# Averages as 32-column tiles on TensorE, and five of twelve key units a batch turned by TensorE instead of by DMA

## The chip, the cores and the metric

The kernel runs on one core of a Trainium2 chip: TensorE (matrix products, into PSUM), VectorE, ScalarE and GpSimd (elementwise work), SyncE, whose queue here issues all DMA transfers, and 16 DMA engines behind it. The metric is the device time of one execution in microseconds; lower is better.

## The reference

Two stages follow one another. The first is two cross-attention layers (16 heads of width 128) and an MLP over `x` [8, 56, 256] with the context `ctx` [8, 1500, 256]. The second, which this text calls the audio stage, is one more cross-attention with 16 heads of width 16 over the same context:

```python
a = layer_norm(audio_kv, ln_gamma, ln_beta)                      # [8, 1500, 256]
Q = (hidden @ Wq.T).reshape(B, 56, 16, 16).transpose(0, 2, 1, 3)
K = (a @ Wk.T).reshape(B, 1500, 16, 16).transpose(0, 2, 1, 3)
V = (a @ Wv.T).reshape(B, 1500, 16, 16).transpose(0, 2, 1, 3)
scores = einsum('bhtd,bhsd->bhts', Q, K) * 16 ** -0.5            # masked, all true here
attn = softmax(scores, axis=-1)
out = einsum('bhts,bhsd->bhtd', attn, V)                         # [8, 16, 56, 16]
result = hidden + tanh(gate) * (out.reshape(B, 56, 256) @ Wo.T)
```

## The kernel before

All products are made in float16 with operands split into a high and a low half, so that most of them are made two or three times.

The audio stage has eight batches. In each, the 16 heads x 56 queries are 896 rows, cut into seven tiles of 128 rows, and the 1500 keys are cut into twelve units of 128. The heads fall into four windows of four heads (224 rows), numbered w = 0 to 3. A unit is one key block's keys and values, 512 columns: six matmuls (`unit`), then `unit_high` on ScalarE and `unit_low` on VectorE write its two halves to the buffer `core`, the values to a ring of 33 slots and the keys to a ring of six.

The program runs tile by tile; tile y = 7 b + s stands in slot s of batch b. In each slot

- TensorE (`audio_attention` in the tensor block) makes the scores of tile y into three PSUM banks SC (six matmuls of 512 columns, twelve where two windows meet, `audio_scores`), then units of the next batch, and in four of the seven slots an average: probabilities times values for one window (`audio_average`);
- VectorE makes the masked minimum of the scores (`audio_minimum`, L1616), the low half of the previous tile's probabilities (`audio_low`, L1634), the low halves of units (L1675) and the softmax scale (L1623, L1625);
- ScalarE converts the previous tile's probabilities (`audio_high`, L1346), picks an average out of PSUM (`pick_average`, L1354), takes the exponential (`audio_exponentiate`, L1337), and makes the high halves of units (`unit_high`, L1330). Two passes over the mask (L1361, L1367) stand in slots 3 and 5;
- the SP queue issues the transposing DMAs: both halves of the previous tile's probabilities (`turn_audio`, L560 and L562, twelve 128 x 128 blocks each), and in slots 0, 2, 4 and 5 the keys of three units of the next batch (`turn_keys`, L551), which the scores need with the key index along the columns; then the loads of the batch after.

The order inside a slot is written out by hand, and each engine runs its own in order. Tables say which slot does what: `SLOT_UNITS` the units, `SLOT_KEYS` the key transposes, `SLOT_WINDOWS` the averages (window 0 in slot 4, 1 in slot 6, 2 and 3 in slots 1 and 2 of the next batch), `SLOT_PICKS` the picks.

An average multiplies 128 value columns (four heads, each with a high and a low half of 16) with all 224 rows of the window. Of the [128, 224] result only four blocks of 32 x 56 are wanted, a head's own columns against its own queries, and a pick reads each with an activation of its own. The averages of windows 0 and 2 go to PSUM bank PV[0], those of 1 and 3 to PV[1].

L791 is the line of the helper `mm`, in which all matmuls are recorded.

## Time and profile before

| what | us |
|---|---|
| median of the three runs (1451.38 to 1454.85) | 1454.21 |
| profiled execution, its own time | 1454.63 |
| its span | 1452.7 |
| audio stage, first minimum to the end | 1126.8 to 1452.7 |
| TensorE busy over the span | 1408.5 (97%) |
| VectorE, ScalarE, GpSimd busy | 988.7, 869.5, 480.2 |

Times in the rows below are from the start of the span. A busy time is a sum of instruction durations, and on TensorE the instructions overlap: the pitch between starts, not the duration of one, is what a matmul takes in a row of them. "Idle before" is the time the engine stood still ahead of a group, with what ended it.

### The profile page before, as it was taken

Reading aid. Unit: us, or ns where it says so; the run is one execution under the profiler, and the core shown is the slowest. Engines: PE = TensorE matmul, PEld = TensorE weight load, DVE = VectorE, ACT = ScalarE, POOL = GpSimd, SP = SyncE. Lnnn points to the kernel's source line nnn. Section 1 sums busy time; section 2 is a strip of 40 time slices with the busy share of each in tenths; the row PEclk is TensorE's granted clock in tenths of the full one; section 3 lists DMA queues with packets and bytes.
Section 4 is the critical chain, followed back from the end, with each engine's and each line's share of the span. In section 5 each row is a group of like instructions: output and inputs, shape, how many; then the busy total and the mean of one; then the engine's idle time right before and its main releaser. Section 6 shows DMA issues by size and latency. Waiting matters only on the chain.

```text
span 1452.7 us, 24712 instructions
## 1 busy us (share of the span) xinstructions
PE 1408.5 (97%) x9188; PEld 888.8 (61%) x9188; DVE 988.7 (68%) x2030; ACT 869.5 (60%) x1566; POOL 480.2 (33%) x393
## 2 busy tenths in 40 slices
PE   9999999999999999999999999999899999999987
PEld 5466666666666654566666666667554455555545
DVE  6866555555555658867666666665657988879886
ACT  6755545545545547655455455455445888988886
POOL 5545433434434200235434433420011443333300
PEclk9999999999999999999999999999999999999999
DMA  6399988889988721599899899987612899999998
GB/s 213 92 228 201 184 171 182 178 171 182 176 173 182 159 88 30 133 219 191 183 178 169 184 177 168 181 163 152 184 41 55 166 219 210 216 209 216 221 199 158
DMA packets 671058, 246.88 MB, mean 170 GB/s; under 512 B 643692, under 2 KB 645212, under 8 KB 670940
## 3 DMA queue, kind: packets, MB, share of 16 engines
q1 hardware_dynamic: 670940, 245.32, 83.4%
q8 instruction: 73, 1.20, 0.3%
q14 instruction: 45, 0.37, 0.1%
HBM read 85.28 MB, written 0.52 MB: 59 GB/s over the span
## 4 chain that ended last, share of the span: by engine, by line
PE 75%; DVE 8%; DMA 7%; ACT 6%; issue 3%; SPq 1%; DVEq 0%; ACTq 0%; POOL 0%; POOLq 0%
PE SC L791 40%; PE PV L791 35%; DMA core<-qc 4%; DVE qc L1634 2%; DVE prob L1616 2%; ACT qc L1346 2%; ACT prob L1337 1%; DMA qc<-core 1%; DVE core L1675 1%; ACT core L1330 1%; DMA core<-core 1%; ACT small L1354 1%; DMA core<-in_wv_dram 1%; ACT rowbuf L1361 0%; SPq L560 0%
## 5 line engine op out<-in xcount | busy, mean ns | idle before, releaser
L791 PE MATMUL PV<-core 128*128 128x256 f16 (+1 forms) x4800 | 540.6, 270 | 14.2 <-DMA core<-qc 6.4
L791 PEld LDWEIGHTS PV<-core 128*128 128x128 f16 x4800 | 458.5, 98 | 83.9 <-issue 15.0
L1278 ACT ACTIVATE prob<-SC,core 128x500 f32<-128x500 f32 x336 | 223.9, 675 | 409.1 <-DVE core L1640 408.4
L791 PE MATMUL SC<-ctxT,qc 128*128 128x500 f16 x2016 | 443.4, 374 | 0.0
L1609 DVE TENSOR_REDUCE mx<-SC 128x1 f32<-128x500 f32 x330 | 220.9, 669 | 316.0 <-PE SC L791 316.0
L791 PEld LDWEIGHTS SC<-ctxT,qc 128*128 128x128 f16 x2016 | 195.9, 97 | 206.9
L719 POOL CAST ctxT<-stage 128x750 f16<-128x750 f32 x64 | 66.9, 1045 | 431.1 <-PE SC L791 223.5
L1667 DVE SCALAR_TENSOR_TENSOR core<-prob,core 128x1500 f16<-128x1500 f32 x112 | 198.4, 1771 | 4.3 <-ACT core L1287 4.3
L1287 ACT ACTIVATE core<-prob 128x1500 f16<-128x1500 f32 x112 | 162.7, 1453 | 3.6
L791 PE MATMUL SC<-ctxT 128*128 128x512 f16 x552 | 131.0, 380 | 4.6 <-DVE core L1675 4.6
L791 PE MATMUL SC<-qc 128*128 128x512 f16 x480 | 114.4, 383 | 12.9 <-DVE mx L1616 12.9
L723 POOL TENSOR_TENSOR core<-stage,core 128x768 f16<-128x768 f32 x64 | 108.0, 1688 | 9.0 <-DVE core L1486 4.1
L1634 DVE SCALAR_TENSOR_TENSOR qc<-prob,rsc,qc 128x1500 f16<-128x1500 f32 x56 | 100.2, 1788 | 10.2 <-ACT qc L1346 8.6
L723 POOL TENSOR_TENSOR ctxT<-stage,ctxT 128x750 f16<-128x750 f32 x64 | 102.9, 1608 | 11.9 <-DVE core L1486 7.1
L719 POOL CAST core<-stage 128x768 f16<-128x768 f32 x64 | 65.2, 1019 | 123.8 <-DMA stage<-in_ctx_nat_dram 122.4
L1616 DVE CUSTOM_DVE_ANT_0 prob<-SC,rowbuf 128x1500 f32<-128x1500 f32 x56 | 95.9, 1713 | 10.4 <-PE SC L791 10.1
L1346 ACT ACTIVATE qc<-prob,rsc 128x1500 f16<-128x1500 f32 x56 | 86.2, 1540 | 22.3 <-DMA core<-qc 12.7
L741 POOL CAST ctxT<-stage 128x768 f16<-128x768 f32 x32 | 26.7, 836 | 216.2 <-PE PV L791 104.2
L791 PEld LDWEIGHTS SC<-ctxT 128*128 128x128 f16 x552 | 53.3, 98 | 69.5 <-DVE core L1675 7.5
L1337 ACT ACTIVATE prob<-prob,mx 128x1500 f32<-128x1500 f32 x56 | 86.4, 1544 | 15.7 <-DVE mx L1616 15.0
L791 PEld LDWEIGHTS SC<-qc 128*128 128x128 f16 x480 | 46.5, 98 | 69.4 <-issue 19.7
L1675 DVE SCALAR_TENSOR_TENSOR core<-SC,rstd,core 128x256 f16<-128x256 f32 x184 | 80.0, 477 | 12.4 <-ACT core L1330 12.3
(147 smaller groups left out, 1332.3 us busy)
## 6 DMA issues: line engine op xcount, KB each, us to landing
stage<-in_ctx_nat_dram SPq DMA_DIRECT2D x64, 384.0 KB, 3.9
stage<-in_ctx_t_dram SPq DMA_DIRECT2D x64, 375.0 KB, 3.4
stage<-in_ctx_p_dram SPq DMA_DIRECT2D x32, 384.0 KB, 4.0
core<-in_wq_dram SPq DMA_DIRECT2D x8, 512.0 KB, 3.5
core<-in_wk_dram SPq DMA_DIRECT2D x8, 512.0 KB, 3.6
core<-in_wv_dram SPq DMA_DIRECT2D x8, 512.0 KB, 5.1
core<-in_wo_dram SPq DMA_DIRECT2D x8, 512.0 KB, 5.0
core<-core SPq DMA_TRANSPOSE x224, 4.1
```

What stands on the lines that cost most here:

```text
L719: nc.gpsimd.tensor_copy(hi, src).then_inc(split_hi, 1)
L723: nc.gpsimd.tensor_tensor(lo, src, hi, ALU.subtract).then_inc(stage_free, 1)
L791: return nc.tensor.matmul(o, a, c, start=start, stop=stop, skip_group_check=skip)
L1278: nc.scalar.activation(prob[:, i, c * CW:c * CW + w], SETS[i][c][:, 0:w], ACT.Exp, bias=nmax[:, i, :], accum_out=sum3[:, i, c:c + 1]).then ...
L1287: nc.scalar.activation(ph[:, i, 0:T], prob[:, i, 0:T], ACT.Copy, scale=UP).then_inc(ph_hi, 1)
L1337: nc.scalar.activation(prob[:, i, 0:T], prob[:, i, 0:T], ACT.Exp, scale=-1.0, bias=mx3[:, i, 0:1], accum_out=sum3[:, i, 0:1]).then_inc(as_ ...
L1346: nc.scalar.activation(aph[:, i, 0:T], prob[:, i, 0:T], ACT.Copy, scale=rsc[:, y % 4, 1:2]).then_inc(aph_hi, 1)
L1609: nc.vector.tensor_reduce(mx3[:, t % 2, c:c + 1], SETS[t % 2][c][:, 0:w], AX_X, ALU.max)\
L1616: nc.vector.tensor_tensor_reduce(out=prob[:, i, 0:T], in0=scores_of(y), in1=maskb[:, b % 2, :], scale=1.0, scalar=3.0e38, op0=ALU.add, op1 ...
L1634: nc.vector.scalar_tensor_tensor(aph[:, i, TC:TC + T], prob[:, i, 0:T], rsc[:, y % 4, 1:2], aph[:, i, 0:T], ALU.mult, ALU.subtract).then_i ...
L1667: nc.vector.scalar_tensor_tensor(ph[:, i, TC:TC + T], prob[:, i, 0:T], UP, ph[:, i, 0:T], ALU.mult, ALU.subtract).then_inc(ph_lo, 1)
L1675: ins = nc.vector.scalar_tensor_tensor(lo[:, i, :, :], src[:, i, :, :], rstd[:, n:n + 1], hi[:, i, :, :], ALU.mult, ALU.subtract)
```

## The change

`audio_average` makes each of the 24 matmuls as four: 32 value columns of one head against that head's 56 probability columns, each into its own 32 PSUM partitions and all into the same 56 columns. So a pick is one activation of 128 x 56. All averages go to PV[0], except those of windows 1 and 3 in the last batch, and each waits for the pick of the one before it (`attn_ready`).

Five units of each following batch (3, 4, 5, 9 and 10; `SLOT_TURN`) have their keys turned by TensorE, in slots 1 to 5: `turn_unit` multiplies the four 128-column pieces of a unit's keys with a float16 identity into PV[1], and `turned_keys` on ScalarE copies the bank to the key store. Their DMA transposes go: of the four of a batch one is dropped (slot 2) and that of slot 5 turns one unit. The identity is made by VectorE during the MLP in the space of a constant that is no longer read. The two passes over the mask move from slots 3 and 5 to 2 and 6, the mask's load from slot 1 to 0.

```diff
+        ident16 = dmean[:, 0:P // 2].bitcast(F16)
...
-        SLOT_KEYS = {0: 0, 2: 1, 4: 2, 5: 3}
+        SLOT_KEYS = {0: 0, 4: 2, 5: 3}
+        SLOT_TURN = {1: 3, 2: 4, 3: 5, 4: 9, 5: 10}
...
+        def average_bank(b, w):
+
+            return PV[w % 2 if b == B - 1 else 0]
...
+                first, count = by_transfer(g)[0], len(by_transfer(g))
+                j = first % NT
+                o = kst[:, b % 2, j:j + count, :, :].rearrange("p j w t -> p (j w) t")
+                sp.dma_start_transpose(o, core16[:, key_slot(first):key_slot(first) + count * UNIT]).then_inc(kt_full[k], 16)
...
-                if s == 1 and b + 1 < B:
+                if s == 0 and b + 1 < B:
                     mask_load(b + 1)
...
+            def turn_unit(n):
+
+                if turns_through(n) == 1:
+                    pe.wait_ge(ident_ready, 1)
+                    pe.wait_ge(aq_lo, NW)
+                else:
+                    pe.wait_ge(kp_full, turns_through(n) - 1)
+                pe.wait_ge(m_lo, n + 1)
+                for w in range(NW):
+                    ins = mm(PV[1][:, w * P:(w + 1) * P], core16[:, key_slot(n) + w * P:key_slot(n) + (w + 1) * P],
+                             ident16, True, True)
+                ins.then_inc(kp_mm, 1)
...
                 y = RT * b + FIRST_TILE[w]
-                if n >= 2:
-                    pe.wait_ge(attn_ready, n - 1)
+                if n >= 1:
+                    pe.wait_ge(attn_ready, n - 1 if b == B - 1 and w > 0 else n)
...
-                        ins = mm(PV[w % 2][:, 0:WR], values(NT * b + j, w)[0:r, :],
-                                 probT[0:r, i * NT + j, w * WR:(w + 1) * WR], j == 0 and i == 0, j == NT - 1 and i == 1)
+                        v = values(NT * b + j, w)
+                        for h in range(HW):
+                            own = slice(2 * KA * h, 2 * KA * (h + 1))
+                            c = w * WR + h * Q
+                            ins = mm(average_bank(b, w)[own, 0:Q], v[0:r, own], probT[0:r, i * NT + j, c:c + Q],
+                                     j == 0 and i == 0, j == NT - 1 and i == 1)
...
                     for n in slot_units(y)[0:1]:
                         unit(n, y)
+                    if turned_unit(y) is not None:
+                        turn_unit(turned_unit(y))
                     if at_slot(SLOT_WINDOWS, y):
                         audio_average(*at_slot(SLOT_WINDOWS, y))
...
+            def turned_keys(n):
+
+                b, j = divmod(n, NT)
+                act.wait_ge(kp_mm, turns_through(n))
+                if b >= 2:
+                    act.wait_ge(as_score, RT * (b - 1))
+                nc.scalar.activation(kst[:, b % 2, j, :, :].rearrange("p w t -> p (w t)"), PV[1][:, :],
+                                     ACT.Copy).then_inc(kp_full, 1)
...
-                for h in range(HW):
-                    own = slice(2 * KA * h, 2 * KA * (h + 1))
-                    ins = nc.scalar.activation(attnT[own, w, b * Q:(b + 1) * Q], PV[w % 2][own, h * Q:(h + 1) * Q],
-                                               ACT.Identity, scale=1.0 / PROB_SCALE, bias=vbias[own, w:w + 1])
-                ins.then_inc(attn_ready, 1)
+                nc.scalar.activation(attnT[:, w, b * Q:(b + 1) * Q], average_bank(b, w)[:, 0:Q], ACT.Identity,
+                                     scale=1.0 / PROB_SCALE, bias=vbias[:, w:w + 1]).then_inc(attn_ready, 1)
...
                     for n in slot_units(y)[0:1]:
                         unit_high(n, y)
-                    if s == 3 and b + 1 < B:
+                    if turned_unit(y) is not None:
+                        turned_keys(turned_unit(y))
+                    if s == 2 and b + 1 < B:
                         mask_row(b + 1, (b + 1) % 2)
-                    if s == 5 and b + 1 < B:
+                    if s == 6 and b + 1 < B:
                         mask_addend(b + 1, (b + 1) % 2)
```

The next rows are TensorE's, from the scores of slot 0 to those of slot 3 in batch 1. First before: the scores are `SC<-qc`, the units `SC<-ctxT`, the averages `PV<-core`.

```order
577 L791 MATMUL SC<-qc 128x512 x6
578 L791 MATMUL SC<-ctxT 128x512 x12
579 L791 MATMUL SC<-qc 128x512 x12
580 L791 MATMUL SC<-ctxT 128x512 x6
581 L791 MATMUL PV<-core 128x224 x24
582 L791 MATMUL SC<-qc 128x512 x6
583 L791 MATMUL SC<-ctxT 128x512 x6
584 L791 MATMUL PV<-core 128x224 x24
585 L791 MATMUL SC<-ctxT 128x512 x6
586 L791 MATMUL SC<-qc 128x512 x12
```

The same place in the changed kernel; `PV<-dmean,core` are the turned keys (the identity lies in `dmean`).

```order
585 L828 MATMUL SC<-qc 128x512 x6
586 L828 MATMUL SC<-ctxT 128x512 x12
587 L828 MATMUL SC<-qc 128x512 x12
588 L828 MATMUL SC<-ctxT 128x512 x6
589 L828 MATMUL PV<-dmean,core 128x128 x4
590 L828 MATMUL PV<-core 32x56 x96
591 L828 MATMUL SC<-qc 128x512 x6
592 L828 MATMUL SC<-ctxT 128x512 x6
593 L828 MATMUL PV<-dmean,core 128x128 x4
594 L828 MATMUL PV<-core 32x56 x96
595 L828 MATMUL SC<-ctxT 128x512 x6
596 L828 MATMUL SC<-qc 128x512 x12
```

The averages stand where they stood, with four times the instructions, and ahead of each in slots 1 and 2 stand four matmuls of the turned unit.

ScalarE from the exponential of slot 1 to that of slot 3, in batch 1, before. L1330 is a unit's high half, L1346 a tile's conversion, L1354 a pick.

```order
762 L1337 ACTIVATE prob,sum<-prob,mx 128x1500
763 L1330 ACTIVATE core<-SC,rstd 128x2x16x16
764 L1346 ACTIVATE qc<-prob,rsc 128x1500
765 L1354 ACTIVATE small<-PV,vbias 32x56 x4
766 L1337 ACTIVATE prob,sum<-prob,mx 128x1500
767 L1330 ACTIVATE core<-SC,rstd 128x2x16x16
768 L1346 ACTIVATE qc<-prob,rsc 128x1500
769 L1330 ACTIVATE core<-SC,rstd 128x2x16x16
770 L1354 ACTIVATE small<-PV,vbias 32x56 x4
771 L1337 ACTIVATE prob,sum<-prob,mx 128x1500
```

And after, with the lines renumbered (L1411 for L1337, L1395 for L1330, L1420 for L1346, L1426 for L1354); L1404 copies turned keys, L1432 is the mask's first pass.

```order
740 L1411 ACTIVATE prob,sum<-prob,mx 128x1500
741 L1395 ACTIVATE core<-SC,rstd 128x2x16x16
742 L1404 ACTIVATE qc<-PV 128x512
743 L1420 ACTIVATE qc<-prob,rsc 128x1500
744 L1426 ACTIVATE small<-PV,vbias 128x56
745 L1411 ACTIVATE prob,sum<-prob,mx 128x1500
746 L1395 ACTIVATE core<-SC,rstd 128x2x16x16
747 L1404 ACTIVATE qc<-PV 128x512
748 L1432 ACTIVATE rowbuf,anym<-mask 128x1500
749 L1420 ACTIVATE qc<-prob,rsc 128x1500
750 L1395 ACTIVATE core<-SC,rstd 128x2x16x16
751 L1426 ACTIVATE small<-PV,vbias 128x56
```

The copy of turned keys stands ahead of each conversion, and so ahead of the pick behind it; a pick is one instruction.

The SP queue, slots 4 and 5 of batch 0, before: the key transposes are L551.

```order
506 L551 DMA_TRANSPOSE qc<-core 128x12x128
507 L560 DMA_TRANSPOSE core<-qc 128x12x128
508 L562 DMA_TRANSPOSE core<-qc 128x12x128
509 L551 DMA_TRANSPOSE qc<-core 128x12x128
510 L560 DMA_TRANSPOSE core<-qc 128x12x128
511 L562 DMA_TRANSPOSE core<-qc 128x12x128
```

After; L588 is the key transpose.

```order
505 L588 DMA_TRANSPOSE qc<-core 128x12x128
506 L597 DMA_TRANSPOSE core<-qc 128x12x128
507 L599 DMA_TRANSPOSE core<-qc 128x12x128
508 L588 DMA_TRANSPOSE qc<-core 128x4x128
509 L597 DMA_TRANSPOSE core<-qc 128x12x128
510 L599 DMA_TRANSPOSE core<-qc 128x12x128
```

Slot 5's key transpose has four blocks instead of twelve; slot 2's, ahead of this piece, is gone.

## Rows read from the trace of the kernel before

**Rows 1.** Stretches: length, busy TensorE, loads, VectorE, ScalarE, GpSimd; granted clock, DMA share, GB/s.
```profile
1163.70:1204.30 40.60, 38.54 (x229) 21.69 (x228) 35.79 (x65) 36.17 (x52) 15.46 (x12) 1.00 1.13 219
...
1245.80:1289.30 43.50, 39.88 (x230) 22.53 (x229) 35.81 (x64) 37.60 (x54) 15.45 (x12) 0.96 1.12 211
1289.30:1328.70 39.40, 38.05 (x230) 21.92 (x229) 35.53 (x63) 34.92 (x52) 15.46 (x12) 1.00 1.13 219
```

**Rows 2.** Groups by form, TensorE: name and shape, count | busy, mean ns | idle before.
```profile
L791 PE MATMUL SC<-ctxT 128*128 128x512 f16 x552 | 131.0, 380 | 4.6 <-DVE core L1675 4.6
...
L791 PE MATMUL PV<-core 128*128 128x224 f16 x704 | 77.6, 261 | 10.6 <-DMA core<-qc 6.4 <-issue 4.1
L791 PEld LDWEIGHTS PV<-core 128*128 128x128 f16 x4400 | 419.3, 98 | 80.0 <-issue 15.0 <-DMA core<-qc 3.9 <-DMA core<-core 1.9
```

**Rows 3.** Timeline of TensorE in batches 3 and 4: start, span in us, name, count.
```profile
1281.80 1.31 PE L791 MATMUL PV<-core 128*128 128x224 f16 x12 [2.33 <-issue]
...
1283.88 2.42 PE L791 MATMUL PV<-core 128*128 128x224 f16 x12 [0.77 <-DMA core<-qc]
...
1288.99 2.75 PE L791 MATMUL SC<-ctxT 128*128 128x512 f16 x12
...
1295.46 2.47 PE L791 MATMUL PV<-core 128*128 128x224 f16 x24
```

**Rows 4.** Table of waits, 1163.7 to 1370: total us, times, longest.
```profile
ACT qc L1346 <- DMA core<-qc: 12.7, 8, 2.5
...
PE PV L791 <- DMA core<-qc: 5.2, 7, 1.1
...
PE PV L791 <- issue: 4.1, 3, 2.3
...
PE SC L791 <- DVE core L1675: 3.0, 7, 0.6
```

**Rows 5.** Timeline of the SP queue in batch 3.
```profile
1270.60 4.22 SPq L562 DMA_TRANSPOSE core<-qc  x1
...
1275.55 1.44 SPq L551 DMA_TRANSPOSE qc<-core  x1
1277.09 2.80 SPq L560 DMA_TRANSPOSE core<-qc  x1
1279.94 1.49 SPq L562 DMA_TRANSPOSE core<-qc  x1
```

**Rows 6.** Timeline: narrow matmuls of the first stage, one-column ones, and these by form.
```profile
20.41 0.35 PE L791 MATMUL SC<-core 128*128 128x448 f16 x1
...
20.69 0.14 PEld L791 LDWEIGHTS SC<-prob,core 128*64 128x64 f16 x4 [0.37 <-DVE core L1486]
20.69 0.57 PE L791 MATMUL SC<-prob,core 128*64 128x448 f16 x4
...
1079.80 0.63 PE L791 MATMUL SC<-dmean,prob 128*112 128x1 f32 x5
...
L791 PE MATMUL SC<-dmean,prob 128*112 128x1 f32 x48 | 5.1, 236 | 0.4 <-ACT prob L1220 0.4
```

**Rows 7.** DMA transposes of four and of twelve blocks: ns on the queue.
```profile
L527 SPq DMA_TRANSPOSE qc<-core x112: 1188/1202/2183, 81.4 to 1030.5; - x112
...
L551 SPq DMA_TRANSPOSE qc<-core x32: 1392/1754/2608, 1080.6 to 1399.3; - x32
```

**Rows 8.** Timeline of ScalarE in slots 1 and 2 of batch 4.
```profile
1297.76 0.67 ACT L1330 ACTIVATE core<-SC,rstd 128x512 f16<-128x512 f32 x1
1298.96 1.54 ACT L1346 ACTIVATE qc<-prob,rsc 128x1500 f16<-128x1500 f32 x1 [0.53 <-DVE rsc L1625]
1300.41 1.22 ACT L1354 ACTIVATE small<-PV,vbias 32x56 f32<-32x56 f32 x4
```

**Rows 9.** Timeline of TensorE at the same place.
```profile
1300.36 2.47 PE L791 MATMUL PV<-core 128*128 128x224 f16 x24
```

More of the change, by code:

```diff
@@ L242, in build @@
         ta_hi = sem("ta_hi")
-        kt_full = [sem(f"kt_full{k}") for k in range(2)]
+        kt_full = [sem(f"kt_full{k}") for k in range(PIECES)]
+        kp_mm = sem("kp_mm")
+        kp_full = sem("kp_full")
+        ident_ready = sem("ident_ready")
         pad_ready = sem("pad_ready")
@@ L401, in slot_units, with turned_unit, turns_through, kt_count @@
             return [NT * (b + 1) + j for j in SLOT_UNITS[s] if 0 <= y and NT * (b + 1) + j < NT * B]
+        def turned_unit(y):
+            b, s = divmod(y, RT)
+            return NT * (b + 1) + SLOT_TURN[s] if s in SLOT_TURN and b + 1 < B else None
+        def turns_through(n):
+            b, j = divmod(n, NT)
+            return TURNS * (b - 1) + 1 + list(SLOT_TURN.values()).index(j)
+        def kt_count(b, k):
+            return 16 * sum(1 for c in range(b + 1) if by_transfer(PIECES * c + k))
+        def by_tensor(n):
+            return n >= NT and n % NT in SLOT_TURN.values()
+        def by_transfer(g):
+            return [n for n in range(JP * g, JP * (g + 1)) if not by_tensor(n)]
         def at_slot(table, y):
@@ L1024, in audio_scores @@
                         for k in range(c, c + 2):
-                            pe.wait_ge(kt_full[k % 2], 16 * (PIECES // 2 * b + k // 2 + 1))
+                            by_pe = [n for n in range(NT * b + JP * k, NT * b + JP * (k + 1)) if by_tensor(n)]
+                            if by_pe:
+                                pe.wait_ge(kp_full, turns_through(by_pe[-1]))
+                            if len(by_pe) < JP:
+                                pe.wait_ge(kt_full[k], kt_count(b, k))
                     o = SC[:, at:at + 512].rearrange("p (j t) -> p j t", t=P)
```

18 lines of the change are left out of this document (13 added, 5 removed).

## The prediction

> **What bounds the kernel now.** I read the table by stretch first, one stretch for each batch of audio tiles [rows 1]. Only the audio stage is changed, 326 us of the profiled execution (1126.8 to 1452.7), so everything before it stays. In batches 1 to 5 (1163.7 to 1370.0, 206.3 us) a batch takes between 39.4 and 43.5 us, TensorE is busy 38 to 40 us in each, VectorE and ScalarE 35 to 38. Busy times overlap at instruction ends, so I went to the groups by form next [rows 2] and priced them by pitch. Twelve matmuls of 512 columns span 2.75 us with one of 0.38, so their pitch is (2.75 - 0.38) / 11 = 0.216 us; 24 of 224 columns span 2.47 with one of 0.26, a pitch of 0.096 [rows 3]. Five batches hold 660 wide matmuls (scores and key/value units) and 480 of the averages: 660 x 0.216 + 480 x 0.096 = 142.6 + 46.1 = 188.7 us. The waits of TensorE in that stretch, from the table of waits, are 5.2 + 4.1 us ahead of averages and 3.0 us elsewhere [rows 4]. That makes 201.0 of 206.3 us; most of the rest is the stretch in which the averages ran at half clock after a gap (twelve in 2.42 us instead of 1.31, batch 3, granted clock 0.96) [rows 1, 3]. So TensorE is the bound, at 91%, and what it waits for in the averages is a transposing DMA: the one row that says "issue" for 2.33 us starts 4.7 us after the SP queue issued the transpose of that tile's high half at 1277.09, and the second half starts 3.94 us after the issue at 1279.94 [rows 3, 5]. The SP queue is behind there: one issue took 4.22 us instead of about 1.8, a key transpose stands between it and the next [rows 5], and the DMA share of the stretch is 1.12 [rows 1]. ScalarE too waits 12.7 us for these transposes [rows 4].
>
> **The averages as narrow tiles.** An average was 24 matmuls (128 columns of values, 224 moving columns), 24 x 0.096 = 2.31 us. It becomes 96 of 32 value columns by 56 moving ones, four in a row on four different column groups. No row has this shape. The nearest is the token score of the first stage, 64 value columns wide, two side by side: four matmuls of 448 columns span 0.57 us, where four one behind the other would need about 0.35 + 3 x 0.19 = 0.92 (0.35 is a wide one's span, 0.19 its pitch by the line through the two above), and four weight loads of 0.11 us span 0.14 [rows 6]. So matmuls on different column groups do run together. The two pitches above give 0.417 ns a column plus 2.7 ns, so 56 columns take 0.026 us. Bounds: all four together, 24 x 0.026 = 0.6 us; one behind the other, 96 x 0.026 = 2.5 us; and far above, if a small matmul never comes faster than the one-column ones of the layer norm (five in 0.63 us with one of 0.24: pitch 0.099) [rows 6], 96 x 0.099 = 9.5 us. I take the middle of the first two, 1.6, since four loads go together but 192 instructions instead of 48 have to be issued. The change of width costs too: the first narrow matmul starts 0.28 us after the wide one before it, whose pitch would be 0.19 [rows 6], so 0.09 us in and as much out, 0.2 an average. Sum 1.8 us, 0.5 less than now: 20 averages in five batches, **-10 us** (between -30 and +8; the far end +148).
>
> The Trainium skill, "TensorE: Matmul & The Clock Gate", section "Back-to-back issue gap", speaks against this change: it puts a floor under small matmuls, about 25 ns each, or 62 ns each where the sequencer decodes them. By 62 ns an average would be 6.0 us and the 32 of them 117 us dearer, some 1570 us in all; by 25 ns they come out at 2.4, no change. The rows have no long run of small matmuls, so they don't decide between the two; they only show two starting together.
>
> **Five key units turned by TensorE.** Each adds four matmuls of 128 columns against the identity: by columns 0.056 us each, by the weight load 0.098 [rows 2]. I take 0.08, so 0.32 us a unit; 25 units in five batches, **+8 us** (+6 to +10). Each also adds a ScalarE copy of 512 columns, like a unit's first half at 0.68 us [rows 8]. ScalarE is paid back: a pick was four activations in 1.22 us and becomes one of about 0.30 [rows 8]. Per batch: 5 x 0.65 - 4 x 0.92 = -0.4 us. VectorE gets nothing but one small copy during the MLP. Neither engine is the bound, so this is nothing in the middle batches.
>
> **What leaves the SP queue.** Of twelve key units a batch, five are no longer turned by DMA: one of four key transposes goes (slot 2), one shrinks from twelve 128 x 128 blocks to four (slot 5). With 14 transposes of twelve blocks for the probabilities that is 216 blocks down to 196, 9% less. On the SP queue a twelve-block issue takes 1.75 us and a four-block one 1.20 [rows 7]; so SP saves 1.75 + 0.55 = 2.3 us a batch. A queue that is late by less than that now and then stops being late. I let 7 of the 9.3 us of DMA waits ahead of averages go, the half-clock stretch behind one of them (a mean granted clock of 0.96 over 43.5 us [rows 1] is 1.7 us lost), and 0.8 of the waits for VectorE, which ScalarE's stalls push back: **-9.5 us** (between 0 and -13). What is late next is VectorE: 35.8 us busy a batch [rows 1].
>
> **A wait that is added.** All averages of batches 0 to 6 now go to one bank, and the turned keys have the other. So an average waits for the pick of the one before. That matters only in slot 2, where the pick of window 2 stands on ScalarE behind the previous tile's conversion and now also behind a turned key. In batch 4 the conversion starts at 1298.96 and the pick at 1300.41; with the turned key (0.58) ahead and one activation instead of four it would be done at about 1298.96 + 0.58 + 1.45 + 0.30 = 1301.3. TensorE reaches that average at 1300.36 today [rows 8, 9], after the added 0.32 at 1300.7. So it waits 0.6; unit 8 and the scores of the next tile are queued behind it, and VectorE's minimum waits for those. I take 0.5 on average, five times: **+2.5 us** (0 to +9, if the pick is always 1.9 late). The moves of the mask's two passes (ScalarE, slots 3 and 5 to 2 and 6) stand behind the exponential and are covered by VectorE's slot.
>
> **Sum.** Five middle batches: -10 + 8 - 9.5 + 2.5 = -9. Batch 6 the same with fewer units: -1.5. Batch 0 has five turns and two averages: +0.5. In the last batch there are no turns; one pick sits between a conversion and an exponential that VectorE then waits for without TensorE being later, -0.9, and the last half average after the last transpose (1.31 us, as [rows 3]) loses 0.2 of it; the shorter last pick gains nothing, since the output's first matmuls run beside it. Together -1.1, or about -11 in all. The profiled execution took 1454.63 us (span 1452.7 and 1.9 around it), 0.4 above the median of 1454.21: 1454.6 - 11.1 = 1443.5, against the median **1443 us**.
>
> **Rivals.**
> 1. Tiles one behind another. If only starts overlap and the array takes the four in turn, an average costs 2.5 + 0.2 = 2.7: +8 + 8 - 9.5 + 2.5 = +9 for the middle batches, +2 for the others, **1465 us**, slower. It decides as soon as an average costs over 2.3 us. For it: TensorE is the bound, so each 0.1 us an average is 3 us in all. Against it: 0.57 instead of 0.92 us for the four narrow ones.
> 2. Bound by the issue of instructions. Today two instructions, a load and a matmul, go in 0.096 us, 0.048 each; the rows don't show that they could go faster for long. 192 x 0.048 = 9.2 us an average, +7 x 32 = +220: **1675 us**. The skill's 62 ns (above) is a milder form of it. Against it: four loads and four matmuls in a window in which only the streaming takes time [rows 6].
> 3. No change. The averages come out near 2.2, or the pick in slot 2 is 1.9 late each time (+9 instead of +2.5): **1452 us**.
> 4. More than forecast. The four tiles run fully together (0.8 with the change of width, -20 more) and the DMA waits go; then VectorE and ScalarE at about 36 to 37 us a batch hold it, some 22 to 24 us under now: **1431 us**.
>
> **Chances.** Forecast 0.53; rival 1 0.12; rival 2 in either form 0.06; rival 3 0.15; rival 4 0.14. What a measurement of this kernel can tell from no change is 0.3%, 4.4 us: faster under 1449.8, slower over 1458.6. Forecast and rival 4 with a little of rival 3 are faster, 0.68; same 0.14; slower 0.18. The range of 1430 to 1459 leaves out rivals 1 and 2 and a tip of rival 4; the forecast's own range is 1435 to 1450.
>
> **What would show it.** In the profile after: 24 groups of four in 1.4 to 1.8 us for an average, the four loads and four matmuls of a group starting together; a group of 128-column matmuls at 0.06 to 0.10 us pitch; TensorE's wait for DMA ahead of averages under 3 us in the middle batches; a new wait of slot 2's average for the pick before it, 0 to 1 us each; middle batches of 39 to 40 us. The forecast is wrong if an average takes over 2.3 us, if the slot 2 wait is near 2 us, or if the transposes are as late as now although the SP queue has less to issue.

## The result

The changed kernel took 1447.44 us (median of 15 runs, 1442.73 to 1453.76), the kernel before beside it 1453.01 us (15 runs, 1451.38 to 1456.51). The ratio is 0.9956, interval 0.9947 to 0.9966: about 6 us faster. The forecast was 1443 us, 11 under the kernel before, with a range of 1430 to 1459. The sign and the range hold, the gain is half of the forecast, and most terms of the sum behind it don't hold.

Profile after: span 1445.4 us, 7.3 less than before. Stretches of the audio stage, columns as in [rows 1]; batches 1 to 5, batch 6, the last batch:

```profile
1162.70:1358.20 195.50, 176.93 (x2682) 86.99 (x2680) 177.11 (x316) 174.24 (x226) 77.27 (x60) 0.98 1.14 211
1358.20:1397.00 38.80, 30.12 (x508) 14.70 (x505) 33.10 (x57) 33.29 (x43) 5.57 (x4) 0.96 1.12 181
1397.00:1445.40 48.40, 31.24 (x662) 17.83 (x662) 29.34 (x40) 25.19 (x29) 0.00 (x0) 0.84 0.92 153
```

The same stretches before:

```profile
1163.70:1370.00 206.30, 193.36 (x1141) 109.66 (x1140) 178.75 (x317) 181.43 (x261) 77.28 (x60) 0.99 1.13 216
1370.00:1407.40 37.40, 32.93 (x204) 19.17 (x201) 33.27 (x58) 34.05 (x49) 5.58 (x4) 1.00 1.17 203
1407.40:1452.70 45.30, 35.37 (x230) 24.03 (x230) 29.23 (x40) 32.21 (x50) 0.00 (x0) 0.96 0.87 164
```

The middle batches gained 10.8 us; batch 6 lost 1.4 and the last batch 3.1, at a granted clock of 0.84 against 0.96. (The rest, 1.0, is the audio stage's earlier start, in a stage that the change doesn't touch; batch 0 takes 36.9 us in both.) TensorE's busy time in the middle batches fell by 16.4 us, and with 176.93 it is now level with VectorE's 177.11.

TensorE's timeline, batch 3, slots 1 and 2, answers to the averages of [rows 3, 9]:

```profile
1248.71 0.39 PE L828 MATMUL PV<-dmean,core 128*128 128x128 f16 x4
1249.03 0.98 PE L828 MATMUL PV<-core 128*32 128x56 f16 x96
1250.04 1.46 PE L828 MATMUL SC<-qc 128*128 128x512 f16 x6
...
1254.00 1.09 PE L828 MATMUL PV<-core 128*32 128x56 f16 x96 [0.99 <-ACT small L1426]
```

An average is 96 matmuls in 0.98 us, and the next scores start 1.01 us after its first. The single records show the four matmuls of a group starting about 3 ns apart and most groups 26 ns apart (some 33 to 43, and 0.11 us between the two halves). 26 ns is the pitch of 56 columns by [rows 3]: the four tiles run fully together. A turned unit is 0.32 us from its start to the average's, 0.09 of it for the change of width: the first narrow matmul starts 0.147 us after the last turn, and the turns are 0.056 apart. Slot 2's average waits for the pick (L1426).

The table of waits, 1162.7 to 1358.2, answers to [rows 4] (total us, times, longest):

```profile
PE PV L828 <- ACT small L1426: 8.1, 5, 2.3
PE PV L828 <- DMA core<-qc: 4.9, 4, 3.3
ACT qc L1420 <- DMA core<-qc: 3.1, 5, 0.9
```

Slots are read off the starts of VectorE's minimum, and numbered from 0. An undisturbed middle batch takes 37.7 us (slots 0 to 6: 5.17, 5.16, 6.2, 5.17, 5.78, 4.79, 5.43). Batch 2 took 41.5 (slot 6: 8.66) and batch 4 40.2 (slot 2: 8.74). Each had a wait with half clock behind it, and here is what that looks like (batch 2, slot 6; then batch 4, slot 2):

```profile
1237.47 0.54 PE L828 MATMUL PV<-core 128*32 128x56 f16 x48 [3.28 <-DMA core<-qc]
1237.95 1.89 PE L828 MATMUL SC<-ctxT 128*128 128x512 f16 x6
1239.63 2.77 PE L828 MATMUL SC<-qc 128*128 128x512 f16 x6
...
1292.64 1.13 PE L828 MATMUL PV<-core 128*32 128x56 f16 x96 [2.27 <-ACT small L1426]
1293.70 2.74 PE L828 MATMUL SC<-ctxT 128*128 128x512 f16 x6
```

Six matmuls of 512 columns take 2.74 to 2.77 us instead of 1.46: the clock is at 1.2 instead of 2.4 GHz, after TensorE stood. In the audio stage after the change the records of the clock hold five such stretches of 3.4 us and one of 10.6 us at the very end; before there were two of 3.4 us.

Batch 6 lost its time in slot 4, 8.35 us instead of 5.99: TensorE stood for 2.21 us after four of twelve scores, with no wait that the profile shows, and half clock followed. The last batch lost it in slot 2, 7.20 us instead of 4.88, and behind the last minimum, 19.1 us instead of 16.9; its other slots are 1.4 us shorter. Slot 2 there has a wait for the pick that the kernel before didn't have, 2.28 us, with half clock behind it.

### The profile page after: what moved, and what is told of

Read it like the earlier page. It is cut to its first block, busy times and chain, and to the rows that moved or that the text cites. A ratio compares the mean times of both kernels' runs of the same rounds, so it can differ in the third digit from the quotient of the medians.

```text
span 1445.4 us, 29611 instructions
## 1 busy us (share of the span) xinstructions
PE 1384.9 (96%) x11632; PEld 854.1 (59%) x11632; DVE 987.6 (68%) x2031; ACT 855.7 (59%) x1505; POOL 478.2 (33%) x393
## 3 DMA queue, kind: packets, MB, share of 16 engines
q8 instruction: 93, 1.52, 0.4%
## 4 chain that ended last, share of the span: by engine, by line
PE 76%; DVE 10%; DMA 5%; issue 4%; ACT 4%; SPq 2%; ACTq 0%; POOL 0%; DVEq 0%; POOLq 0%
PE SC L828 41%; PE PV L828 34%; DMA core<-qc 3%; DVE qc L1707 3%; DVE prob L1689 3%; DVE core L1748 2%; ACT qc L1420 1%; DMA core<-core 1%; ACT core L1395 1%; DMA core<-in_wv_dram 1%; ACT rowbuf L1438 0%; DVE core L1740 0%; SPq L597 0%; ACT prob L1411 0%; SPq L599 0%
## 5 line engine op out<-in xcount | busy, mean ns | idle before, releaser
L828 PE MATMUL PV<-core 128*128 128x256 f16 (+1 forms) x7104 | 492.6, 238 | 24.8 <-ACT small L1426 11.8
L828 PEld LDWEIGHTS PV<-core 128*128 128x128 f16 (+1 forms) x7104 | 414.5, 96 | 91.8 <-ACT small L1426 14.8
L1740 DVE SCALAR_TENSOR_TENSOR core<-prob,core 128x1500 f16<-128x1500 f32 x112 | 201.3, 1797 | 6.4 <-ACT core L1349 6.3
L828 PE MATMUL SC<-ctxT 128*128 128x512 f16 x552 | 134.8, 383 | 4.4 <-DVE core L1748 4.3
L828 PE MATMUL SC<-qc 128*128 128x512 f16 x480 | 118.9, 394 | 19.6 <-DVE mx L1689 17.1
L760 POOL TENSOR_TENSOR core<-stage,core 128x768 f16<-128x768 f32 x64 | 105.1, 1643 | 9.0 <-DVE core L1559 4.1
L1411 ACT ACTIVATE prob<-prob,mx 128x1500 f32<-128x1500 f32 x56 | 86.5, 1545 | 33.2 <-DVE mx L1689 32.2
L1420 ACT ACTIVATE qc<-prob,rsc 128x1500 f16<-128x1500 f32 x56 | 86.4, 1544 | 9.6 <-DVE rsc L1698 5.6
```

The costliest lines, as they stand in the source:

```text
L760: nc.gpsimd.tensor_tensor(lo, src, hi, ALU.subtract).then_inc(stage_free, 1)
L828: return nc.tensor.matmul(o, a, c, start=start, stop=stop, skip_group_check=skip)
L1411: nc.scalar.activation(prob[:, i, 0:T], prob[:, i, 0:T], ACT.Exp, scale=-1.0, bias=mx3[:, i, 0:1], accum_out=sum3[:, i, 0:1]).then_inc(as_ ...
L1420: nc.scalar.activation(aph[:, i, 0:T], prob[:, i, 0:T], ACT.Copy, scale=rsc[:, y % 4, 1:2]).then_inc(aph_hi, 1)
L1740: nc.vector.scalar_tensor_tensor(ph[:, i, TC:TC + T], prob[:, i, 0:T], UP, ph[:, i, 0:T], ALU.mult, ALU.subtract).then_inc(ph_lo, 1)
```

## The experiments

Each was timed beside the kernel before (its medians 1453.2 to 1454.4), and the ratios are to that. Times are medians; a trace is of one execution, and where that one was far from the median, the text says so.

### Each half of the change alone

`narrow_only`, the kernel before with narrow averages and the single pick, every key unit still turned by DMA:

```
-   ins = mm(PV[w % 2][:, 0:WR], values(...)[0:r, :], probT[0:r, i * NT + j, w * WR:(w + 1) * WR], ...)
+   for h in range(HW):
+       ins = mm(PV[w % 2][own, 0:Q], v[0:r, own], probT[0:r, i * NT + j, c:c + Q], ...)
...
-   for h in range(HW):
-       ins = nc.scalar.activation(attnT[own, w, ...], PV[w % 2][own, h * Q:(h + 1) * Q], ...)
+   nc.scalar.activation(attnT[:, w, ...], PV[w % 2][:, 0:Q], ...)
```

> The kernel before with one half of the change: averages as 96 matmuls of 32 x 56 and one activation for a pick, in two PSUM banks by turns as before; all keys still turned by DMA. Theory A (TensorE was the bound and the DMA queue comes next): TensorE sheds 1.3 us an average, but its waits for DMA ahead of averages (9.3 us in batches 1 to 5) and ScalarE's (12.7 us) stay or grow, so the middle batches take 39 to 40 us and the whole about 1446 to 1449 us. Rival (the shed TensorE time is all gained, down to VectorE's 36 us a batch): about 1430 us. Rival (a lighter TensorE falls to half clock more often and gives all of it back): 1452 us or more, with a granted clock of 0.98 or less.

Measured: **1463.56 us** (5 runs), ratio 1.0061 (1.0048 to 1.0073). Cheaper averages alone make the kernel slower. Middle batches and the last batch, then the waits of the middle ones:

```profile
1161.70:1377.40 215.70, 177.46 (x2579) 82.95 (x2578) 178.55 (x316) 163.66 (x203) 77.18 (x60) 0.94 1.16 210
...
1412.40:1457.80 45.40, 29.85 (x662) 17.38 (x662) 29.31 (x40) 25.22 (x29) 0.00 (x0) 0.84 1.00 174
```
```profile
ACT qc L1350 <- DMA core<-qc: 25.1, 14, 2.5
PE PV L791 <- DMA core<-qc: 24.3, 17, 3.5
...
PE PV L791 <- issue: 7.2, 6, 2.0
```

TensorE is 16 us less busy than before and the stretch 9 us longer: the wait for transposed probabilities grew from 5.2 [rows 4] to 24.3 us and the clock fell to 0.94. (The traced execution took 1459.75 us, the fastest of the five.) The last batch lost nothing, 45.4 against 45.3 us, although its clock was 0.84 too.

`wide_turned`, the changed kernel with wide averages and four picks again:

```
-   ins = mm(average_bank(b, w)[own, 0:Q], v[0:r, own], probT[0:r, i * NT + j, c:c + Q], ...)
+   ins = mm(average_bank(b, w)[:, 0:WR], values(...)[0:r, :], probT[0:r, i * NT + j, w * WR:(w + 1) * WR], ...)
...
-   nc.scalar.activation(attnT[:, w, ...], average_bank(b, w)[:, 0:Q], ...)
+   for h in range(HW):
+       ins = nc.scalar.activation(attnT[own, w, ...], average_bank(b, w)[own, h * Q:(h + 1) * Q], ...)
```

> The changed kernel with the averages wide again (24 matmuls of 128 x 224, four activations for a pick), still in one bank and with the five turned units. Theory A (narrow averages carry the gain): TensorE has 1.3 us more in each of 32 averages and 0.3 us in each of 35 turns than the kernel before or after, so about 1460 us, over the kernel before. Rival (the shorter DMA queue carries the gain): the waits for DMA fall as in the changed kernel and the time is about 1447 to 1450 us.

Measured: **1459.19 us** (6 runs), ratio 1.0040 (1.0026 to 1.0054).

```profile
1162.30:1368.40 206.10, 195.94 (x1242) 115.76 (x1240) 177.72 (x316) 193.50 (x286) 77.22 (x60) 1.00 1.04 201
```
```profile
1251.08 2.47 PE L828 MATMUL PV<-core 128*128 128x224 f16 x24
1253.39 1.46 PE L828 MATMUL SC<-qc 128*128 128x512 f16 x6
...
1258.21 2.48 PE L828 MATMUL PV<-core 128*128 128x224 f16 x24 [1.84 <-ACT small L1424]
```

All five middle batches are 41.2 us to 0.02, no average waits for a DMA and the clock stays at 1.00, but it is no gain: the turns and a pick wait of 1.84 us cost what the DMA waits did. This is the trace of the fastest of the six executions, 1455.74 us; the others lie between 1456.9 and 1462.9 at a clock of 0.995 to 0.998 instead of 1.000, so the even 41.2 us may not hold for them. The DMA share is 1.04 against 1.13 before, with 9% fewer blocks to turn in the same time. So neither half gains alone (+9.4 and -0.2 us in the middle batches of the traces), together they gain 10.8. The reading that fits is that narrow averages need probabilities on time, and that the turned keys help to bring them and need the room on TensorE. From this kernel to the changed one slots 0 and 2 fall from 6.3 and 8.47 to 5.17 and 6.2; the others stay, and VectorE at 35.4 us a batch is right behind. Of 4 x 1.2 us saved a batch (the average's 2.31 us became 1.1), 3.5 come through.

### The wait for the pick

`pick_early`, the changed kernel with slot 2's pick moved on ScalarE ahead of the conversion:

```
+   if s == 2 and at_slot(SLOT_PICKS, y):
+       pick_average(*at_slot(SLOT_PICKS, y))
    if 0 < y <= RT * B:
        audio_high(y - 1)
...
-   if at_slot(SLOT_PICKS, y):
+   if s != 2 and at_slot(SLOT_PICKS, y):
```

> The changed kernel with one activation moved: in slot 2 ScalarE picks window 2 before it converts the previous tile, not behind it. Theory B (the added wait for the pick costs): TensorE's wait in slot 2 (8.1 us in batches 1 to 5) goes to under 2 us, slot 2 falls from 6.2 to 6.9 us to about 5.3 to 5.8, seven times, and one half-clock stretch behind such a wait goes: about 1440 us. Rival (VectorE's work is what sets slot 2, so the wait is hidden): no change, 1446 to 1448 us.

Measured: **1445.74 us** (5 runs), ratio 0.9948 (0.9936 to 0.9960), not told apart from the changed kernel. The 8.1 us of pick waits are gone and undisturbed batches take 37.3; in their place stand waits for DMA, the longest in slot 6 of batches 2 and 5 (slots of 8.68 and 9.43 us). The middle batches:

```profile
1164.20:1362.60 198.40, 176.85 (x2678) 86.95 (x2676) 178.09 (x315) 175.79 (x228) 77.21 (x60) 0.97 1.16 210
```
```profile
PE PV L828 <- DMA core<-qc: 13.3, 12, 3.3
```

The last batch, with the pick wait of its slot 2 at 0.32 us:

```profile
1398.30:1443.90 45.60, 29.81 (x662) 17.59 (x662) 29.33 (x40) 25.29 (x29) 0.00 (x0) 0.85 1.00 165
```

So 2.8 of the 3.1 us that the last batch lost come back by the place of one pick, at the same low clock. What was gained there and in batch 6 (35.7 us) the middle batches gave away, 198.4 us instead of 195.5.

### What makes the transposes late

`narrow_light`, the kernel `narrow_only` with fewer key blocks sent. It leaves out a part of the computation: from the third batch on, four of a batch's twelve key units aren't turned by anything, so that the scores use older keys and the result isn't the reference's.

```
+   units = 1 if b >= 2 and k % 2 else JP
...
-   sp.dma_start_transpose(o, core16[:, at:at + JP * UNIT])
+   sp.dma_start_transpose(o, core16[:, at:at + units * UNIT])
```

> The kernel with narrow averages and every batch of keys turned by DMA took 1463.56 us, with 25 us of waits for DMA on TensorE and 25 us on ScalarE and eight half-clock stretches. Here its key transfers for the third batch and later are cut: in slots 2 and 5 one unit of three is sent (12 units a batch become 8), nothing is put in their place on TensorE, and the keys of the units left out keep older values (part of the computation is left out). Theory 1, it is the bulk on the transpose queue that makes the turned probabilities late, so that TensorE stands and then runs at half clock: the DMA waits fall to 5 us or less, the middle batches to 37.5 to 39 us, the time to 1440 to 1447 us. Theory 2, it was the matmuls of the turned units that kept TensorE's clock up and covered the waits, and the transfers matter little: the DMA waits stay above 15 us, the time 1455 to 1465 us.

Measured: **1452.52 us** (12 runs), ratio 0.9997 (0.9985 to 1.0009): 11 us of the 16 between `narrow_only` and the changed kernel, with nothing added on TensorE. The averages' waits for DMA went from 24.3 to 17.6 us in five batches, where theory 1 expected 5 or less; the time lies between the two theories. So the transfers are a good part of it, not all. It makes the transfers smaller and still issues all four of a batch, where the changed kernel issues three; whether the 5 us left between them come from that issue or from the turned units on TensorE isn't settled. (The 16.4 us quoted in the expectations is of a stretch 10 us shorter.)

`narrow_light_one`, the same (with the same part left out) with the averages in one bank, so that slot 2 waits for its pick:

```
-   if n >= 2:
-       pe.wait_ge(attn_ready, n - 1)
+   if n >= 1:
+       pe.wait_ge(attn_ready, n - 1 if b == B - 1 and w > 0 else n)
-   ins = mm(PV[w % 2][own, 0:Q], ...)
+   ins = mm(PV[w % 2 if b == B - 1 else 0][own, 0:Q], ...)
```

> The kernel with narrow averages and light key transfers (8 of 12 units sent, none turned; 1452.52 us, 16.4 us of waits of the averages for DMA), with the averages of all batches but the last in one bank, so that slot 2 waits for the pick as in the changed kernel. Theory, that wait (about 1.5 us a batch) holds TensorE back to where the probabilities are ready: the DMA waits fall from 16.4 to 8 us or less and the time to 1446 to 1450 us, although a wait was added. Rival, the wait comes on top and TensorE's matmuls of the turned units are what was missing: DMA waits stay above 12 us, 1453 to 1460 us.

Measured: **1453.31 us** (12 runs), ratio 0.9996 (0.9985 to 1.0008): an added wait for nothing. The waits only change their name:

```profile
PE PV L792 <- ACT small L1357: 11.8, 5, 3.0
...
PE PV L792 <- DMA core<-qc: 5.9, 5, 3.5
```

17.6 became 11.8 + 5.9. The theory had the waits right and the time wrong: that TensorE is held back in slot 2 by a pick instead of by the probabilities changed nothing in the time.

`keys_behind`, the changed kernel with one transfer moved in SyncE's program:

```
-   if s in SLOT_KEYS and b + 1 < B:
+   if s in SLOT_KEYS and s != 5 and b + 1 < B:
        turn_keys(...)
    if y > 0:
        turn_audio(y - 1)
+   if s == 5 and b + 1 < B:
+       turn_keys(...)
```

> The changed kernel with one line of SyncE's program moved: in slot 5 the transfer of unit 11's keys is issued behind the two transposes of the probabilities instead of ahead of them. The bytes and the number of transfers stay. Theory 1, the DMA waits of slot 6's average (4.9 us in the middle batches) come from the place in SyncE's queue, one transfer of 1.5 to 2.6 us ahead of the probabilities: they go as with six turned units (0.2 us), the middle batches stay at 37.7 us but for the bank wait, the time 1441 to 1444 us. Theory 2, it is the load of the DMA engines as a whole: waits of 3 us or more in one or two batches as before, 1446 to 1449 us. Rival against both, the keys now come late for the next batch's slot 0 and slots of 8 us turn up there: over 1449 us.

Measured: **1448.14 us** (11 runs), ratio 0.9969 (0.9957 to 0.9982), no better. The rival was right about where the wait goes, though not about the time:

```profile
PE SC L830 <- DMA qc<-core: 8.8, 5, 2.7
PE PV L830 <- ACT small L1428: 5.1, 5, 1.1
PE PV L830 <- issue: 3.8, 2, 3.6
PE PV L830 <- DMA core<-qc: 1.3, 1, 1.3
```

The averages' 4.9 us fell to 1.3, and the next batch's scores waited 8.8 for the keys, five times. (3.3 of the 4.9 us are one wait, so the first number says less than the second.) The SP queue (start, us on the queue) holds work without a gap there:

```profile
1232.54 1.80 SPq L597 DMA_TRANSPOSE core<-qc  x1
1234.39 3.14 SPq L599 DMA_TRANSPOSE core<-qc  x1
1237.62 1.22 SPq L588 DMA_TRANSPOSE qc<-core  x1
```

`six_turned`, the changed kernel with unit 11 turned by TensorE too, so that slot 5 sends no keys:

```
-   SLOT_KEYS = {0: 0, 4: 2, 5: 3}
-   SLOT_TURN = {1: 3, 2: 4, 3: 5, 4: 9, 5: 10}
+   SLOT_KEYS = {0: 0, 4: 2}
+   SLOT_TURN = {1: 3, 2: 4, 3: 5, 4: 9, 5: 10, 6: 11}
```

> The changed kernel with unit 11 turned by TensorE too, in slot 6, so that slot 5 sends no keys by DMA any more (one transpose of one unit a batch less, one turn of 0.39 us and one copy on ScalarE a batch more). Theory 1, the last DMA waits of slot 6 (3.3 us each) come from what the queue still carries: they go from all middle batches, no batch has a slot 6 over 6 us, and the time falls by the two or three such slots: 1440 to 1444 us. Rival, the turn in slot 6 lies on the path to the next batch's first scores (they wait for the ScalarE copy): slot 6 grows by 0.5 to 1 us in every batch, 1448 to 1453 us. Rival, the lateness is of the probabilities' own transfer: waits as before, 1446 to 1449 us.

Measured: **1442.62 us** (6 runs), ratio 0.9929 (0.9914 to 0.9944). Theory 1 holds for the waits and the time. Its rival holds for slot 6 alone, which is 5.9 us (once 6.2) instead of 5.43; the steady 38.1 to 38.5 us of a batch beat 37.7 with two or three long slots.

```profile
1163.60:1354.90 191.30, 174.20 (x2699) 87.14 (x2698) 176.85 (x316) 176.28 (x231) 77.26 (x60) 1.00 1.13 213
...
1391.30:1439.60 48.30, 30.88 (x662) 17.89 (x662) 29.33 (x40) 25.16 (x29) 0.00 (x0) 0.83 0.84 154
```

The row of averages waiting for DMA is gone from TensorE's waits, its clock is 1.00 up to the last batch, and the DMA share (1.13) is what it was before. So it isn't a lower load of the DMA engines that did this. With `keys_behind` it points to the place in the SP queue, but the turn in slot 6 also makes TensorE come 0.5 us later to what it waited for, and no run tells the two apart.

### The half clock

`fill_tail`, the changed kernel with filler matmuls whose results nothing reads, in the last batch alone:

```
+   def fill(count, bank):
+       for _ in range(count):
+           mm(bank, ident16, wkv[:, 0, 0, :], True, True)
...
+   if y == RT * (B - 1):
+       pe.wait_ge(m_lo, NT * B)
+   if RT * (B - 1) <= y < RT * B:
+       fill((7, 3, 3, 7, 3, 7, 3)[y - RT * (B - 1)], TB[1])    # behind the scores
...
+   if y >= RT * B:
+       fill((4, 6, 2)[y - RT * B], S[1])                       # around the last averages
```

> The changed kernel with extra matmuls (identity times 512 columns of weights, results read by nobody) where TensorE stands still in the last batch: 3 or 7 behind the scores of each tile, 4, 6 and 2 around the last averages. Theory C (a TensorE that stands still runs at half clock behind it, and that is what the tail lost): granted clock of the last batch from 0.84 to 0.95 or more, the last stretch from 48.4 to about 45 us, in all about 1444 us. Rival (the tail is bound by VectorE, ScalarE and the transposes, and the clock costs nothing there): 1447 us, or 1450 if the extra matmuls are in the way.

Measured: **1442.46 us** (4 runs), ratio 0.9922 (0.9909 to 0.9935). Work that nobody needs made the kernel 5 us faster than the changed one (1447.44 us; the two intervals don't meet). The last batch:

```profile
1396.50:1442.30 45.80, 36.10 (x700) 20.44 (x700) 29.31 (x40) 25.15 (x29) 0.00 (x0) 0.93 0.95 163
```

The same scores in the changed kernel and here:

```profile
1398.89 4.44 PE L828 MATMUL SC<-qc 128*128 128x512 f16 x12 [3.46 <-DVE mx L1689]
...
1410.06 4.17 PE L828 MATMUL SC<-qc 128*128 128x512 f16 x12
```
```profile
1398.36 2.75 PE L828 MATMUL SC<-qc 128*128 128x512 f16 x12 [1.95 <-DVE mx L1704]
...
1407.76 2.76 PE L828 MATMUL SC<-qc 128*128 128x512 f16 x12
```

Two of three half-clock stretches went (4.44 and 4.17 us became 2.75 and 2.76); the one over the output remained in this run. Slot 0 fell from 6.35 to 4.66 us and slot 2 from 7.20 to 5.72. In the last batch of the changed kernel TensorE waits five times for VectorE (9.6 us, the longest 3.5), once for the pick (2.3) and at the end for the last transposes (4.5 in all, the longest 3.1). The trace shows 2.6 of the 5 us in the last batch; it is of the slowest of the four executions, 1444.07 us, and the rest can't be placed. The low clock alone doesn't explain the loss: `narrow_only` and `pick_early` have 0.84 and 0.85 there and take 45.4 and 45.6 us. What the changed kernel has beyond them is the wait for the pick with half clock behind it. `wide_turned` waits 3.11 us for that pick at full clock and takes 45.7. So it is the wait and the half clock together, and the early pick or the fillers take away either.

`early_fill_mid`: the pick moved, the fillers of the last batch, and six fillers more between the halves of slot 6's average, where the late probabilities are waited for. Its base is `early_fill`, the first two alone.

```
+   if w == 1 and i == 1 and b < B - 1:      # between the halves of slot 6's average
+       pe.wait_ge(kp_full, TURNS * (b + 1))
+       fill(6, PV[1][:, :])
```

> The changed kernel with both the pick of slot 2 ahead of ScalarE's conversion (1445.74 us alone) and the filler matmuls in the last batch (1442.46 alone). If the two are independent, the differences add: 1440 to 1442 us. Rival, the time won in slot 2 is paid back in slot 6, where TensorE comes earlier to probabilities that come no earlier (13.3 us of DMA waits when alone): 1442 to 1446 us, with slots of 8 to 9 us.

Measured: **1443.68 us** (6 runs), ratio 0.9936 (0.9920 to 0.9953). The two differences didn't add, as the rival had it. Both had shortened slot 2 of the last batch, and together they get that batch to 45.1 us, little under either alone. Slots of 8.46 and 9.23 us stood in slot 6 of batches 2 and 5, and one of 10.79 us in slot 4 of batch 3, where TensorE stops for 3.66 us with no wait that the profile shows. (The traced execution was the slowest of the six, 1447.59 us.)

> The kernel with the early pick and the fillers of the last batch (1443.68 us; slots of 8.5 and 9.2 us after DMA waits in slot 6 at batches 2 and 5, with 3.4 to 6.8 us of half clock behind them), with six filler matmuls of 512 columns (1.3 us at full clock) between the high and the low half of slot 6's average in batches 0 to 6, where TensorE waits for the low probabilities. Theory 1, the clock is a good part of what such a wait costs: the half-clock stretches behind slot 6 go, its late slots are 7 us or less, the time 1437 to 1442 us. Theory 2, lateness alone sets these slots and the fillers are in the way in the others: late slots stay over 8 us, the others grow by up to 1 us, 1444 to 1451 us.

Measured: **1444.78 us** (6 runs), ratio 0.9931 (0.9914 to 0.9948), no change. The trace looks like theory 1: no half clock in batches 0 to 5, late slots of 6.6 to 7.7 us. The time is theory 2's: other slots grew. In the middle batches, where TensorE is 90% busy, the fillers took back what the clock gave; they paid only in the last batch, where TensorE has nothing else to do.

### Together

`six_fill` is `six_turned` with `fill_tail`; `six_early_fill` has the early pick as well.

> The changed kernel with six turned units (1442.62 us alone, middle batches all 38.1 to 38.5 us, no wait of TensorE for DMA) and the filler matmuls of the last batch (about 5 us alone), and the pick of slot 2 in its old place. If the steady middle batches and the held clock of the end are independent: 1436 to 1439 us, with no slot of the middle batches over 7 us, so steadier than with the early pick too (1436.02, six slots of 7 to 9 us in its trace). Rival, fillers and turns crowd the instruction stream: stops at instruction blocks of 3 us come, 1440 to 1444 us.

Measured: **1439.64 us** (6 runs, 1438.44 to 1443.93), ratio 0.9907 (0.9889 to 0.9925), between both theories. The last batch is 43.5 us at full clock, below the 45.3 before; two slots of about 8 us are back in the middle:

```profile
1161.70:1356.60 194.90, 176.89 (x2699) 87.63 (x2698) 176.87 (x315) 177.81 (x233) 77.39 (x60) 0.98 1.13 210
...
1393.10:1436.60 43.50, 34.83 (x704) 18.86 (x702) 29.25 (x40) 25.23 (x30) 0.00 (x0) 1.00 0.96 171
```
```profile
1236.43 0.98 PE L828 MATMUL SC<-ctxT 128*128 128x512 f16 x3 [2.69 <-issue]
1237.21 2.77 PE L828 MATMUL SC<-qc 128*128 128x512 f16 x6
```

> Everything together: six turned units, the early pick of slot 2, fillers in the last batch. If the waits of slot 6 hang on the keys that the queue still carries, all middle batches stay at 37.3 to 37.8 us and the time is 1434 to 1439 us. Rival, the early pick still runs into late probabilities: two to four slots of 8 to 9 us remain, 1440 to 1446 us.

Measured: **1436.02 us** (6 runs, 1434.52 to 1443.42), ratio 0.9889 (0.9870 to 0.9909). The best version, 17 us under the kernel before and 11 under the changed one. Its profiled run was its slowest (1443.42) and shows 9.2 us of DMA waits and three slots of 7.2 to 8.8 us, as the rival said (three, not the six that the expectation of `six_fill` names); the other five took 1434.5 to 1437.0, as the theory said.

### What the long waits have in common

Instructions come over DMA queues of their own, and `q8 instruction` of the page carries blocks of 16 KB (1.52 MB in 93) whose number grows with TensorE's instructions. The five middle batches hold 9 such blocks before, 10 in `wide_turned`, 20 in `narrow_only` and 21 in the changed kernel. While a block moves and just behind it, the transposes mostly stand still. The next rows are of the changed kernel, columns as in [rows 1], the last one GB/s: 1 us ahead of the block that starts at 1235.47, 1 us from 1235.8 on, and 1 us around the end of the 3.28 us wait of batch 2 (1237.47):

```profile
1234.40:1235.40 1.00, 0.00 (x0) 0.00 (x0) 1.00 (x1) 1.00 (x2) 0.82 (x1) 1.00 1.10 207
1235.80:1236.80 1.00, 0.00 (x0) 0.00 (x0) 0.00 (x0) 1.00 (x1) 0.00 (x0) 1.00 0.92 8
1237.20:1238.20 1.00, 0.73 (x50) 0.60 (x51) 0.77 (x1) 1.00 (x3) 0.00 (x0) 1.00 1.28 275
```

Over the 21 blocks of its middle batches the rate falls from 227 GB/s in the 1 us before a block to 73 GB/s between 0.4 and 1.2 us after its start. And in the audio stages of all fourteen traces, all 17 waits of an average for a DMA of 2.5 us or more have the start of such a block in them (mostly 1.9 to 2.4 us before TensorE goes on), but only 5 of the 46 waits of 0.9 to 2.5 us. So the late slot 6 of batch 2 (8.66 us here, 8.68, 8.46 and 8.30 in `pick_early`, `early_fill` and `six_early_fill`) is no chance of the queue: a block stands at that place of the program. This is a rival to the account by the SP queue, and no run here tests it. It can't be the whole: of the 24.3 us of `narrow_only` three waits with a block in them are 9.4, and the other 15 us have none.

## Why the prediction was right in sign and range and wrong in its terms

- **An average at 1.8 us.** 1.1 us with the change of width. The two bounds were 0.6 and 2.5 plus 0.2, and I took the middle, because 192 instructions have to be issued. The row that I read as "they run together" [rows 6] meant just that; the pitch of 26 ns a group is the lower bound. So twenty averages saved 24 us (1.2 each), not 10: the largest error of the sum. The Trainium skill's floor ("TensorE: Matmul & The Clock Gate", section "Back-to-back issue gap", 62 or 25 ns a matmul) doesn't fit the trace: 96 matmuls and 96 loads start within 1.01 us, 10.5 ns a matmul. The measurement decides, and rivals 1 and 2 fall.
- **Turns, +8.** 0.39 us a unit with 0.32 to the average that follows: right.
- **DMA waits, -9.5.** Of the 9.3 us that I counted (5.2 for DMA and 4.1 under "issue") 4.9 are left, so 4.4 went instead of 7. ScalarE's went from 12.7 to 3.1, and TensorE's for VectorE's units from 3.0 to 2.2, the 0.8 that I had. But the half clock, 1.7 us that I let go, became two stretches instead of one, 1.7 us more. So the term is -3.5. The step that failed is the reasoning that fewer blocks on the queue make it punctual while the demand stays: the batches became 5% shorter, the DMA share came back to 1.14, and with narrow averages and all keys on the queue these waits are 24.3 us (`narrow_only`). Two terms were missing, that a faster TensorE asks for the probabilities sooner, and that four times the instructions bring twice the instruction blocks; what each is worth isn't told apart.
- **The bank wait, +2.5.** 8.1 us, five waits of 1.6, near the end of my range. Yet moving the pick away gained nothing in the middle batches (`pick_early`): other waits took its place there.
- **VectorE is late next.** Right: undisturbed batches of 37.7 us, 35.4 of them VectorE. Of rival 4 the first half came true, that the four tiles run fully together, and the second did not, that the DMA waits go.
- **Batch 6 at -1.5, the last batch at -1.1.** +1.4 and +3.1. Batch 6 has one stop of 2.21 us in mid-scores with half clock behind it, for which the sum has no term. In the last batch the step that failed is that the added wait is priced in the middle batches only: window 3 of batch 6 is averaged in slot 2 of the last batch, waits 2.28 us for the pick there, and the twelve scores behind it take 4.17 us at half clock instead of 2.75. The sum has no wait there, and every span at full clock. `narrow_only`, without that wait, loses nothing in its last batch (45.4 us); `pick_early` gets 2.8 of the 3.1 us back, the fillers of `fill_tail` 2.6, and `six_fill` is at 43.5.

Against the forecast of -11: middle batches -10.8 instead of -9, batch 0 and start -1.0 (all of it the earlier start) instead of +0.5, batch 6 +1.4 instead of -1.5, last batch +3.1 instead of -1.1; together -7.3 in the profiled executions and -5.6 in the medians. For the middle batches the terms as measured are -24 + 8 - 3.5 + 8.1 = -11.4; waits for VectorE's minimum, 0.5 before and 2.7 after, make it -9.2 of the -10.8, and the rest isn't placed. That the forecast of -9 came near it is luck: an average cheaper by 14 us than forecast stood against a bank wait 5.6 us and DMA waits 6 us dearer.

Still open: why TensorE stops in mid-stream with no semaphore involved (below), and whether the instruction blocks make the transposes late or only go with it.

## What to carry to other kernels

When one engine is made lighter, add up again what its work had covered: a queue that was just in time turns late, and a clock that was held falls. A wait that a change adds must be priced at every place where it stands, the last batch too. Test the parts of a change alone and together; here each part alone was a loss and both a gain. And count instruction blocks when a change multiplies instructions. Where an engine idles in short waits at the end of a kernel, filler work of no use can be worth several us; where TensorE was 90% busy it brought nothing here.

## What the runs showed of the hardware

- Four matmuls on 32-column tiles start about 3 ns apart and groups of four follow at 26 ns for 56 columns in most places. The change from full to narrow tiles costs 0.09 us, as it did in [rows 6].
- In the changed kernel's audio stage each half-clock stretch begins 0.4 to 1.5 us after TensorE is back from a wait of 2.2 to 3.5 us, so it falls on the matmuls that come next. Such a wait doesn't always bring it: `wide_turned` waits 3.46 and 3.11 us in its last batch and keeps full clock until 1452.1 of 1453.5.
- A block of 16 KB on the instruction queue goes with a stop of the transposing DMAs: 8 GB/s for 1 us instead of 207 (above).
- TensorE stops for 2 to 3.7 us in mid-stream with "issue" as the reason. In `fill_tail`, `early_fill` and `keys_behind` it is after 86 of the 96 matmuls of the same average, slot 4 of batch 3, for 3.23, 3.66 and 3.59 us. `fill_tail`:

```profile
1264.12 0.98 PE L828 MATMUL PV<-core 128*32 128x56 f16 x86
1268.33 0.27 PE L828 MATMUL PV<-core 128*32 128x56 f16 x10 [3.23 <-issue]
```

In all three the queue of instruction blocks starts one block of 16 KB in that time, 2.5 to 2.6 us before TensorE goes on. In the page it is `q8 instruction: 93, 1.52, 0.4%` where before it was 73, in `narrow_only` 91 and in `wide_turned` 75: 96 instructions in the place of 24 make for more blocks. The Trainium skill ("Advanced Engine Details and Errata", section "ISA Cache") gives a block of 16 KB as 256 instructions; the row agrees on the size (1.52 MB in 93). By that figure the 72 more matmuls and 72 more weight loads of each of 32 averages are 18 blocks, an estimate, and `narrow_only` has 18 more than the kernel before. That a stop comes from a late block is argued from these coincidences, and no run here tests it.
